# A graph and attention network on one core: scores of the middle attention as two products over 128 partitions in place of three over 64, and probabilities turned by ordinary fp32 products

## The reference

```python
x = x + gnn(xn, edge_index, W_l, W_r, b) + linear_attention(xn, W_qkv, W_proj, b_proj)
x = x + middle_attention(layernorm(x))        # the stage of the change
x = x + edge_messages(xn, ...) + linear_attention_2(xn, ...)
x = x + anchors_ffn(layernorm(x), ...)

def gqa(x, wq, wk, wv, wo, n_kv):
    scores = jnp.einsum('bhqd,bhkd->bhqk', q, k) / jnp.sqrt(jnp.float32(D_K))
    attn = jax.nn.softmax(scores, axis=-1)
    out = jnp.einsum('bhqk,bhkd->bhqd', attn, v)
    return out.transpose(0, 2, 1, 3).reshape(B, S, D_MODEL) @ wo
```

## Time and profile before

| | |
|---|---|
| runs shown | 2628.89, 2633.79, 2633.82 us, median 2633.79 |
| profiled execution | 2621.18 us, span 2619.2 us |
| TensorE, VectorE, ScalarE, GpSimd busy | 94%, 69%, 35%, 63% of the span |
| stretch of the middle attention's items | about 414 to 553 us |
| the last stage (anchors, from about 960 us) | TensorE's products L1698 to L1700 without a break |

### The profile page before, as it was taken

The page is one execution under the profiler, slowest core; times in us unless marked ns, Lnnn a source line. Parts: engine busy times, 40 slices in busy tenths (PEclk is TensorE's granted clock), DMA queues, the critical chain, the costliest instruction groups (busy, mean ns, idle before and its releaser), DMA issues.

```text
span 2619.2 us, 34595 instructions
## 1 busy us (share of the span) xinstructions
PE 2457.5 (94%) x11680; PEld 2056.2 (79%) x11680; DVE 1802.2 (69%) x2675; ACT 924.4 (35%) x1128; POOL 1649.6 (63%) x724
## 2 busy tenths in 40 slices
PE   6989978976899679999999999999999999999999
PEld 6878877865799667777777777777777777777777
DVE  8974324547588657777777777777777777777775
ACT  3732224522389552223223232223222322322231
POOL 0024322228888745777777777777777777777773
PEclk9989877988799779999999999999999999999999
DMA  3024010011433200221212212122122221221211
GB/s 77 16 68 162 17 65 17 1 49 47 110 87 92 79 38 33 97 84 76 96 64 96 95 65 96 69 91 96 64 96 80 80 96 64 96 91 69 96 64 36
DMA packets 49889, 190.90 MB, mean 73 GB/s; under 512 B 13300, under 2 KB 17911, under 8 KB 33444
## 3 DMA queue, kind: packets, MB, share of 16 engines
q1 hardware_dynamic: 35728, 177.90, 19.4%
q0 software_dynamic: 13200, 10.75, 1.9%
q10 hardware_dynamic: 900, 1.44, 0.2%
HBM read 177.54 MB, written 12.35 MB: 72 GB/s over the span
## 4 chain that ended last, share of the span: by engine, by line
PE 79%; DVE 10%; POOL 6%; issue 2%; ACT 2%; DMA 1%; SPq 0%; DVEq 0%; ACTq 0%; POOLq 0%
PE PS L1698 25%; PE PS L1700 25%; PE PS L1699 25%; POOL gatW L751 3%; POOL XN L751 2%; PE PS L1776 2%; DVE hotS L1151 1%; POOL gat L751 1%; DVE hotD L1152 1%; DVE negmax L1388 1%; DVE PTl L1405 1%; PE PS L1962 1%; PE PS L1920 0%; PE PS L1963 0%; DVE XN L1115 0%
## 5 line engine op out<-in xcount | busy, mean ns | idle before, releaser
L1648 DVE SCALAR_TENSOR_TENSOR XN<-PS,attn,XN 125x512 f32<-125x512 f32 x1083 | 805.4, 749 | 439.9 <-PE PS L1700 431.4
L789 POOL TENSOR_TENSOR OPl<-TS,OPh 128x1024 fp32r<-128x1024 f32 x256 | 677.5, 2647 | 116.7 <-ACT OPh L1061 116.7
L789 POOL TENSOR_TENSOR OPl<-RAW,OPh 128x1024 fp32r<-128x1024 f32 x192 | 555.2, 2892 | 273.4 <-ACT OPh L1061 273.4
L1698 PE MATMUL PS<-OPh,XTh 128*125 128x512 f32 x1280 | 507.6, 397 | 2.0 <-DVE attn L1602 2.0
L1700 PE MATMUL PS<-OPh,XTl 128*125 128x512 f32 x1280 | 506.1, 395 | 0.0
L1699 PE MATMUL PS<-OPl,XTh 128*125 128x512 f32 x1280 | 503.7, 394 | 0.0
L1061 ACT ACTIVATE OPh<-TS 128x1024 fp32r<-128x1024 f32 x256 | 271.8, 1062 | 530.0 <-PE PS L1700 517.3
L1061 ACT ACTIVATE OPh<-RAW 128x1024 fp32r<-128x1024 f32 x192 | 203.8, 1062 | 579.1 <-PE PS L1700 579.1
L1698 PE MATMUL PS<-OPh,Sh 128*125 128x512 f32 x1024 | 404.3, 395 | 3.1 <-DVE XN L1645 3.1
L1700 PE MATMUL PS<-OPh,Sl 128*125 128x512 f32 x1024 | 403.4, 394 | 0.0
L1699 PE MATMUL PS<-OPl,Sh 128*125 128x512 f32 x1024 | 402.1, 393 | 0.0
(11 more groups left out here) (345 smaller groups left out, 3587.6 us busy)
## 6 DMA issues: line engine op xcount, KB each, us to landing
RAW<-in_values SPq DMA_DIRECT2D x64, 2048.0 KB, 7.5
filters<-filt SPq DMA_DIRECT2D x14, 672.0 KB
fil<-filters SPq DMA_DIRECT2D x11, 840.0 KB
Wraw<-in_ffn SPq DMA_DIRECT2D x4, 1024.0 KB, 5.3
Wraw<-in_L_q SPq DMA_DIRECT2D x2, 1024.0 KB, 5.1
Wraw<-in_L_k SPq DMA_DIRECT2D x2, 1024.0 KB, 8.7
Wraw<-in_L_v SPq DMA_DIRECT2D x2, 1024.0 KB, 7.3
gatW<-nodes,dstI POOLq DMA_INDIRECT x90
```

Of the source, the lines that this page charges most:

```text
L789: g.tensor_tensor(OPl[:, j], operand_source(j, parity), OPh[:, j].bitcast(F32), ALU.subtract).then_inc(op_lower, 1)
L1648: v.scalar_tensor_tensor(out=XN[:, t], in0=PS[0:P, bank, :], scalar=w, in1=XN[:, t], op0=ALU.mult, op1=ALU.add).then_inc(v_added, 1)
L1698: mm(dst, lh, rh, start=start, stop=False, skip_group_check=resumed)
```

## The change

Queries are kept in one buffer, `queries_both`: for each of the eight heads, partitions 0 to 63 hold the upper part and 64 to 127 the lower part. `keys_high` holds a head's upper part twice, in both halves of the partitions, and `keys_low` (in two buffers, heads 0 to 3 in the place of XN, heads 4 to 7 behind `prob`) the lower part twice. A score is then two products over 128 partitions: queries_both by keys_high, and queries_both by keys_low; it also takes in lower by lower, which was left out before. To write them, ScalarE copies 64 partitions at a time, two pieces for a unit of queries and four for a unit of keys, and so does VectorE. The transposes of `prob` become ordinary matmuls in fp32 with the identity as the moving operand.

```diff
-            for stage, dst, scale in (("q1", QFh, DH ** -0.5), ("k1", KFh, 1.0)):
-                for f in range(K):
-                    u = (stage, f)
-                    wait_filled(u)
-                    upper(u, halves(dst[:, f]), slot(u)[:, :, 0:HN], scale)
-                weight_upper(WEIGHT["F_v" if stage == "q1" else "F_o"])
+            for f in range(K):
+                u = ("q1", f)
+                wait_filled(u)
+                a.activation(halves(queries_both[0:64, 2 * f]), slot(u)[0:64, :, 0:HN], ACT.Copy, scale=DH ** -0.5)
+                upper(u, halves(queries_both[0:64, 2 * f + 1]), slot(u)[64:128, :, 0:HN], DH ** -0.5)
+            weight_upper(WEIGHT["F_v"])
+            for f in range(K):
+                u = ("k1", f)
+                wait_filled(u)
+                a.activation(halves(keys_high[0:64, 2 * f]), slot(u)[0:64, :, 0:HN], ACT.Copy)
+                a.activation(halves(keys_high[64:128, 2 * f]), slot(u)[0:64, :, 0:HN], ACT.Copy)
+                a.activation(halves(keys_high[0:64, 2 * f + 1]), slot(u)[64:128, :, 0:HN], ACT.Copy)
+                upper(u, halves(keys_high[64:128, 2 * f + 1]), slot(u)[64:128, :, 0:HN])
+            weight_upper(WEIGHT["F_o"])
...
-            for stage, up, dst, scale in (("q1", QFh, QFl, DH ** -0.5), ("k1", KFh, KFl, 1.0)):
...
+            for f in range(K):
+                u = ("q1", f)
+                dve.wait_ge(upper_ready, splits(u))
+                for i in range(2):
+                    ins = v.scalar_tensor_tensor(out=halves(queries_both[64:128, 2 * f + i]), in0=slot(u)[64 * i:64 * i + 64, :, 0:HN],
+                                                 scalar=DH ** -0.5, in1=halves(queries_both[0:64, 2 * f + i]).bitcast(F32),
+                                                 op0=ALU.mult, op1=ALU.subtract)
+                ins.then_inc(drained_v, 1)
+            for f in range(K):
+                u = ("k1", f)
+                dve.wait_ge(upper_ready, splits(u))
+                for i in range(2):
+                    for o in (0, 64):
+                        ins = v.tensor_tensor(halves(keys_low(2 * f + i)[o:o + 64]), slot(u)[64 * i:64 * i + 64, :, 0:HN],
+                                              halves(keys_high[o:o + 64, 2 * f + i]).bitcast(F32), ALU.subtract)
+                ins.then_inc(drained_v, 1)
...
-                        ins = product(slot(u)[0:P, h, 0:HN], (QFh[o:o + 64, r, c], QFl[o:o + 64, r, c]),
-                                      (KFh[o:o + 64, r, keys], KFl[o:o + 64, r, keys]), True, True)
+                        mm(slot(u)[0:P, h, 0:HN], queries_both[:, head, c], keys_high[:, head, keys], start=True, stop=False)
+                        ins = mm(slot(u)[0:P, h, 0:HN], queries_both[:, head, c], keys_low(head)[:, keys], start=False, stop=True)
...
-                        ins = nc.tensor.transpose(dst, prob[:, turned % 4, tile_columns(t)], ident[0:P, 0:P])
+                        ins = mm(dst, prob[:, turned % 4, tile_columns(t)], ident[0:P, 0:P], start=True, stop=True)
```

More of the change, by code:

```diff
@@ L190, in build @@
         X = sb("X", [P, T, D], F32)
+        with ExitStack() as s:
+            keys_low_a = sb("keys_low_a", [128, HEADS // 2, NT], F32R, s)
         XN = sb("XN", [P, T, D], F32)
@@ L296, in build @@
         with ExitStack() as s:
[L297 to L300, removed]
+            queries_both = sb("queries_both", [128, HEADS, NT], F32R, s)
+            keys_high = sb("keys_high", [128, HEADS, NT], F32R, s)
             VFh = sb("VFh", [P, T, D], F32R, s)
@@ L305, in build @@
             prob = sb("prob", [P, 4, NT], F32, s)
+            keys_low_b = sb("keys_low_b", [128, HEADS // 2, NT], F32R, s)
         with ExitStack() as s:
@@ L476, in slot, with keys_low @@
             return PS[:, 2 * SLOT[unit]:2 * SLOT[unit] + 2, :]
+        def keys_low(head):
+            return (keys_low_a if head < HEADS // 2 else keys_low_b)[:, head % (HEADS // 2)]
         def name_of(w):
@@ L1891, in _ @@
                     item = n
-                    u, r, o = ("score", item), item // T // 2, 64 * (item // T % 2)
+                    u, head = ("score", item), item // T
                     begin(u)
```

## The result

| | before | changed |
|---|---|---|
| median of 20 runs each | 2632.75 us (2626.07 to 2644.18) | 2622.11 us (2613.08 to 2634.23) |
| ratio, 95% interval | | 0.9962 (0.9951 to 0.9974) |
| profiled execution | 2621.18 us | 2634.23 us |
| first score to first product of the output projection (**S** below) | 141.1 us | 132.2 us |

The changed kernel is faster by 0.38%, 10.0 us by the ratio, within 6.8 to 12.9. The one profiled execution of it happens to be among its slowest. The two profiles therefore can't be compared by their spans; they can be by a stretch. S is such a stretch: it holds all of the items and heads, and it went from 554.84 - 413.77 = 141.1 us to 557.86 - 425.62 = 132.2 us, 8.8 us less.

The account below looks back on a forecast made before the run. It took TensorE's middle attention, partly at half clock, to bound the kernel. Head 0 3.5 us earlier, 1.1 us more per further phase and a full-clock last head made 4.4 us saved: 2629.4 us, range 2621 to 2640.

Parts of the forecast that it names:

- More falls before: Rival: in timed runs most phases end in a clock fall that the change removes; about 10.5 us saved, 2623; chance 0.2.
- main case: Middle attention: 4.4 us saved, own range 1.5 to 8 us; chance 0.64.
- What bounds the kernel, and the cover: Middle attention bounds; writing operands in pieces costs nothing, covered by 9 us of value projection.
- Head 0: First phase: clock back at 425.4 us in place of 444.3, value products at 435.2, 3.5 us earlier.
- The heads: Each further phase at full clock takes 1.1 us more, bounds 0.6 and 1.3; a head is then 15.87 us.
- The last phase and the last head: Head 7 starts at 544.2 against 547.25 and takes 4.63 us at full clock, ending at 548.8 against 553.25.
- The clock: From 420.61 us, products over 125 or 128 partitions raise it in 4.8 us; it should not fall at a phase's end.
- The clock does not follow: Rival: all clock falls in the middle attention stay; 9.5 us more, 2643.3; chance 0.12.
- A factor of four: Rival: turning products take four times a transpose's 0.11 us; 45 us more than the sum, 2674; chance 0.02.

Follow-up runs that it names:

- e3: Kernel before with only the turning changed, transposes of the probabilities made ordinary products, scores still three over 64 partitions: S 153.5 us, ratio 1.0043 to the kernel before.
- e2: Changed kernel with the transposes put back, so only the scores differ from the kernel before: S 123.5 us, ratio 0.9938 to the kernel before.
- e9: The kernel with only the scores changed, profiled once more without a further edit: S 125.3 us, ratio 0.9946 to the kernel before.
- e5: Scores-only kernel with the first product done twice, its first result overwritten, so three products over 128 partitions: S 127.1 us, one run.
- e6: Kernel before with 30 products over 128 partitions put in front of the first transposes: S 135.3 us, ratio 0.9977 to the kernel before.
- e1: The kernel before profiled once more, no edit: S 142.0 us against 141.1 in its first profile.

## Why the prediction was right or wrong

The forecast was 2629.4 us, 4.4 less, in a range of 2621 to 2640; measured was 2622.1 in the same runs in which the kernel before took 2632.75. The direction was right; the size is half of what came in S (8.8 us), and less than half of the 10.0 us by the ratio. The range holds it only by its lower end, which was put there for the rival of more falls. The main case's own range ended at 8 us saved, so that the range held is luck in part.

**What bounds the kernel, and the cover.** Right. The copies in pieces cost nothing: the last key piece of VectorE ended at 416.35 us and the first score came at 425.62.

**Head 0.** "They start at 435.2, 3.5 us earlier": the value products came 14.23 us after the first turning, 3.85 us earlier than the 18.08 before. Two errors cancel: the clock came back after 6.0 us and not 4.8, and the steps were cheaper than I priced them (a turning 2.09 us at half clock and a score 1.19, not 2.4 and 1.33).

**The heads.** "1.1 us more" failed: it is 0.44 (15.2 against 14.76), and over six heads this makes 4.0 us of the 4.4 that the sum lacked. The term that was mis-sized is "0.74 becomes 1.29, the pair 1.19 becomes 2.29". The records of 0.11 us are right, and e3 measures just these numbers, 1.29 and 2.27, with the old scores behind them. With the new scores they are 1.01 to 1.09 and 2.10. I had priced the two parts of the change each beside the other part's old form; together they also save 0.2 to 0.3 us at each change from the turning of one item to a score, where the next product has 128 rows and not 64. e2 shows the same without the ordinary products: 0.54 in place of 0.74. This moves the limit: a turning and a score now take 1.68 to 1.76 us, not the 2.04 of the sum, and VectorE needs 1.76 us an item. So its maxima follow each other as before behind a head's first (1.76, 2.28, 1.76, 1.76 us against 1.75, 2.23, 1.80, 1.76), where the sum had 0.5 us more, and all that is left of the price is that the first one comes 0.4 to 0.5 us later.

**The last phase and the last head.** Head 6 to head 7 was put at 4.43 + 8.84 + 0.5 = 13.77 us and was 13.77. How much of this hit is luck is open: the last 3.7 of the 8.84 us ran at half clock before, which the sum did not take into account, and no run shows the old phase at full clock. That head 7 would run at full clock was right.

**The clock.** Right that it comes back in head 0's phase and falls behind none. The reason was half wrong. I gave it to both parts, since both are products over full rows and transposes had failed to raise it. e2 and e9 have the transposes and it comes back, in 2.8 and about 6 us; e3 has the products and it does not. It is the rows of the scores, as e5 shows with the count kept. The row on which I relied, ordinary fp32 products that brought the clock back in 4.8 us, was true of a stream of nothing else, and I carried it over to one that is a mixture.

**What I did not ask.** Whether each part of the change pays for itself. The sum had the price of the turning in it, but took the clock as what is bought with it. It buys nothing here: it costs 12.4 us on the kernel before (S 153.5) and 7 to 9 us beside the new scores (132.2 against 123.5 and 125.3). The change's gain of 8.8 us in S is 17.5 of the scores less 8.7 of the turning.

**The rivals.** *More falls before* gives nearly the measured gain, and is not its cause: the second profile of the kernel before has as many falls as the first and an S only 1.0 us longer. *The clock does not follow* fell with the first profile. *A factor of four* too: 20 records in 2.10 us are 0.21 us a product, against 0.09 to 0.15 for a transpose. The Trainium skill's rule of four (TensorE: Matmul & The Clock Gate, section Terms) is not borne out by this; what was measured is about two. The same page of the Trainium skill says, in Part 4: PE-mode transpose, that the full clock does not engage for transposes, which do not count as busy in the same way. The rows here fit that as far as 4.4 us of transposes alone stayed at 0.50, but e2 shows that they do not stand in the way either, when the products among them have full rows.

**Open.** Why ordinary products with 64-row scores keep the clock up but don't bring it back, and how much of that is the identity's zeros, was not tried. Nor was what takes the 0.2 to 0.3 us at a change to a 64-row product. Why half rows count for less with the clock is not shown either, only that they do.

## What to carry to other kernels

Where TensorE is busy and yet granted 1.2 GHz, look at how many rows its products fill: stacking the split operands so that three products over 64 partitions become two over 128 was worth about 14 us with the rows alone, most of it through the clock, and 2 to 3.5 us through the product saved. When a change has two parts, price each beside the new form of the other, and run each alone; here one part took back half of what the other gave. And where whole executions differ by more than the effect, compare a stretch with fixed borders.

## What the hardware showed that I had not expected

- The clock has a memory in both directions. Three half-row products a half with transposes kept 1.00 for 11.8 us by themselves and for 41.6 us with value products in between (e6), and did not bring it back in 18 us (before, e1); half-row scores with ordinary products, and value products in between, kept it for 120.1 us and did not bring it back in the 23.3 us of head 0's first phase (e3).
- The clock can fall while TensorE works without a break. In e6 it fell 2.6 us into half-row scores that stood behind a wait of 1.46 us; with full-row scores at the same place it held for 5.9 us and more.
- A step from turning to a score costs 0.2 to 0.3 us more if the score's products span 64 partitions and not 128: 0.74 against 0.54 us behind transposes, 1.29 against 1.01 to 1.09 behind ordinary products; for a pair 0.17 us more in both cases.
- Of the same kernel before, one execution has 0.83 and another (e1) 0.68 of the clock from 200 to 220 us. The first scores of these two lay 8.2 us apart.
